# First layer of a two-layer decoder on one core: VectorE's second norm moved behind the next pair's masks, and ScalarE's first exponentials behind two copies

## The chip, the core and the metric

The kernel runs on one core of one Trainium2 chip. The metric is the device time of one execution in microseconds (us); the span of a profile runs from the first to the last recorded instruction. PE is TensorE (PEld its weight loads), DVE is VectorE, ACT is ScalarE, POOL is GpSimd, and SP is the engine whose queue issues most of the transfers.

## The reference, cut to what matters

Two decoder layers work on 32 sequences of 64 tokens with 256 channels. Only the first two blocks of the first layer matter here:

```
x = layernorm(x + L0_attn(x))        # local, causal: 16 heads; q and k centred and normed per head;
                                     # scores squared, masked, times v, divided by their sum
x = layernorm(x + L0_xattn(x, ctx))  # cross: q and k RMS-normed, softmax over each sequence's 64
                                     # context positions, times v, output projection with bias
x = layernorm(x + L0_ffn(x))         # 16 routed experts of which 4 are used, 2 shared ones
```

The second layer follows: grouped causal attention, a cross attention with 32 heads, and a mixture of 8 experts with 2 used.

## The kernel before, in words

Everything is f32. `layer0` works through 2048 tokens in 8 pairs of 128-token tiles, and in 10 rounds. Round i does three pairs at once: the local attention of pair i (`la(i)`), the cross attention of pair j = i - 1 (`xa(i)`), and the router's part of pair i - 2 (`router(i)`). All three exist in rounds 2 to 7. Round 1 has no router part, and rounds 8 and 9 have no local attention. A block barrier ends the layer; then the router decides and the expert stage begins.

The order of work on each engine is written out by hand, and the engines meet at semaphores only. Score tiles (for the local and for the cross attention) share four PSUM banks `SB`; two banks `OB` take the weighted sums; all projections and transposes go in turn through two banks `PJ` (class `Banks`), each of which has to be emptied by the engine named in `emptier` before it is filled again. `fill[i, s]` lists the projections that are done ahead for a later group of two pairs in round i at one of four places (`inputs(i, 0)` to `inputs(i, 3)`). The local queries `la_q` and keys `la_k` stand in rounds 0, 2 and 4, the local values `la_v` and the context's keys in rounds 1, 3 and 5, and `kv` tiles for the second layer in rounds 2, 4, 6 and 7. The "query rounds" of the change are those with `la_q` in `fill[i, 0]`; with cross attention there are two of them, rounds 2 and 4.

What one round does around the change, by engine:

- PE: the local scores of pair i into `SB` (line 166, `l_KL` and `l_QM`), `inputs(i, 0)`, a wait for the masks (`ls_used`), the cross scores of pair j (line 166, `l_QX` and `l_KX`), the transposes of the normed pair i - 2 for the router (`r_xtr`, line 834; they wait for `ln2_done` and for a `PJ` bank), the local weighted sums (line 879; they wait for the squared weights), `inputs(i, 1)`, the transposes of O, the router's logits, the local output projection (line 59, `l_wo`), `inputs(i, 2)` and the transposes of the cross weights (line 900; they wait for the exponentials), `inputs(i, 3)`, the cross weighted sums (line 925), the next queries, the cross output projection, the query sums (line 132), and then the local scores of the next round.
- DVE: the masks of pair i, four products of 128x512 (line 676, `l_W`), `inputs(i, 0)`, half of the cross softmax (lines 665 and 666), the outputs of the local attention, `inputs(i, 1)`, the other half, the router's logits, residual and moments, the first norm, the outputs of the cross attention, residual and moments, the query sums (lines 713 and 714), and last the second norm of pair j (`apply(j, 1, ...)`, line 657), which waits for POOL's root (`ln2_root`, line 398).
- ACT: squares of the masked scores (line 514), `inputs(i, 0)` (for `la_q` lines 471 and 473), the copy of `r_xtr` (line 495), the exponentials of the first two banks (`exps(j, (0, 1))`, line 505), `inputs(i, 1)` (for `la_k` lines 479 and 480), the copy of the turned O (line 524), `inputs(i, 2)`, and the other exponentials.
- POOL: at the end of the round the root for the query sums (line 439) and then the root of the second norm (lines 397 and 398).

Of the kernel before, what the change touches and what calls it, by code (L numbers as in the profile page):

```python
# [170 lines left out]
def layer0(nc, es, io, fx):  # L171
# [5 lines left out]
    def inputs_of(g):  # L177
        return {name: [(name, g, i) for i in range(n)] for name, n in
                (("la_q", 2), ("la_k", 2), ("la_var", 1), ("la_v", 2), ("xa_k", 2), ("xa_ks", 1), ("xa_kb", 1),
                 ("xa_v", 2))}  # L180

    fill = {(i, s): [] for i in range(-1, ROUNDS) for s in range(4)}
    for g in range(GROUPS):
        n, i = inputs_of(g), 2 * (g - 1)
# [38 lines left out]
    def la(i):  # L223
        return i < PAIRS

    def xa(i):
        return 0 <= i - 1 < PAIRS

    def router(i):
        return 0 <= i - 2 < PAIRS  # L230
# [21 lines left out]
    def count(name, per=1, step=1):  # L252
        return Count(es, nc, "l0_" + name, per, step)
# [10 lines left out]
    ln1_done, ln2_done = count("ln1_done", 2), count("ln2_done", 2)  # L264
    ln1_stats, ln2_stats, ln1_root, ln2_root = (count(n) for n in ("ln1_stats", "ln2_stats", "ln1_root", "ln2_root"))
# [3 lines left out]
    with ExitStack() as mem:  # L269
# [36 lines left out]
        with nc.Block() as block:  # L306
# [138 lines left out]
            def _(act):  # L445
# [47 lines left out]
                def turned_pair(use, dst):  # L493
                    pj.wait_full(act, use)
                    nc.scalar.activation(dst.rearrange("p m (t q) -> p t m q", t=2),
                                         pj.bank(use)[:].rearrange("p (t m q) -> p t m q", t=2, m=KC),
                                         ACT.Copy).then_inc(pj.emptied["A"], 1)

                def exps(j, which):
                    act.wait_ge(q_root.sem, q_root.at(j))  # L500
                    for r in which:
                        act.wait_ge(xs_used.sem, xs_used.at(j, r))
                        for t in range(2):
                            part = WX[:, r, t * PTOK:(t + 1) * PTOK]
                            last = nc.scalar.activation(part, part, ACT.Exp, scale=qs[:, j % 2, t:t + 1])
                        last.then_inc(xw_ready.sem, 1)

                inputs(-1, 0)
                for i in range(ROUNDS):
                    j = i - 1  # L510
                    if la(i):
                        for r in range(RG):
                            act.wait_ge(ls_used.sem, ls_used.at(i, r))
                            nc.scalar.activation(W[:, r], W[:, r], ACT.Square).then_inc(lw_ready.sem, 1)  # L514
                    inputs(i, 0)
                    if router(i):
                        turned_pair(("r_xtr", i - 2), XTA[:, :, (i - 2) * PTOK:(i - 1) * PTOK])
                    if xa(i):
                        exps(j, (0, 1))
                    inputs(i, 1)  # L520
                    if la(i):
                        use = ("la_otr", i)
                        pj.wait_full(act, use)
                        nc.scalar.activation(OT[:].rearrange("p a (c q) -> p c a q", c=2 * PER),
                                             pj.bank(use)[:].rearrange("p (c a q) -> p c a q", c=2 * PER, a=2),
                                             ACT.Copy).then_inc(pj.emptied["A"], 1)
                    inputs(i, 2)
                    if xa(i):
                        exps(j, (2, 3))
                        for r in range(RG):  # L530
                            act.wait_ge(pt_full.sem, pt_full.at(j, r))
                            nc.scalar.activation(WT[:, r].rearrange("p c q -> p (c q)"), SB[r][:],
                                                 ACT.Copy).then_inc(pt_used.sem, 1)
                    inputs(i, 2, True)
                    inputs(i, 3)
                    if la(i):
                        turned_pair(("xa_xtr", i), XT[:])
                    if xa(i):
                        turned_pair(("xa_otr", j), OT2[:])
                    if la(i):  # L540
                        use = ("xa_q", i)
                        pj.wait_full(act, use)
                        for m in range(KC):
                            got = pj.bank(use)[:, m * PTOK:(m + 1) * PTOK]
                            nc.scalar.activation(SQQ[:, m, :], got, ACT.Square, bias=cols[:, 0, m:m + 1])
                            last = nc.scalar.activation(QX[:, m, :], got, ACT.Identity, bias=cols[:, 0, m:m + 1])
                        last.then_inc(pj.emptied["A"], 1)

            @block.vector
            def _(dve):  # L550
# [102 lines left out]
                def apply(p, n, rooted, done):  # L653
                    dve.wait_ge(rooted.sem, rooted.at(p))
                    for t in range(2):
                        x = X[:, 2 * p + t, :]
                        nc.vector.tensor_scalar(x, x, mv[:, n, t, 0:1], rs[:, n, t:t + 1], ALU.subtract,
                                                ALU.mult).then_inc(done.sem, 1)
# [12 lines left out]
                for i in range(ROUNDS):  # L671
                    j = i - 1
                    if la(i):
                        dve.wait_ge(ls_full.sem, ls_full.at(i))
                        for r in range(RG):
                            nc.vector.tensor_tensor(W[:, r].rearrange("p (c q) -> p c q", q=SEQ),  # L676
                                                    SB[r][:].rearrange("p (c q) -> p c q", q=SEQ),
                                                    fx.cmask[:].unsqueeze(1).broadcast_to([P, 8, SEQ]),
                                                    ALU.mult).then_inc(ls_used.sem, 1)
                    inputs(i, 0)  # L680
                    if xa(i):
                        softmax(j, (0, 1))
                    if la(i):
                        g = i // 2
                        outputs(i, lo_full, lo_done, lambda t: O[:, t, :].rearrange("p (s j d) -> p j s d", s=2, d=16),
                                lambda t: dq[:, g % 2, 2 * (i % 2) + t].rearrange("p (j s) -> p j s", s=2))
                    inputs(i, 1)
                    if xa(i):
                        softmax(j, (2, 3))
                    if router(i):  # L690
                        use = ("r_logit", i - 2)
                        pj.wait_full(dve, use)
                        own(dve, nc.vector.transpose(sums[:, 0:2 * QUAD], pj.bank(use)[:, 0:2 * QUAD]))
                        nc.vector.tensor_copy(
                            fx.LG[:, pair_tiles(i - 2), :],
                            sums[:, 0:2 * QUAD].rearrange("p (t k) -> p t k", k=QUAD)[:, :, 0:E0]).then_inc(pj.emptied["D"], 1)
                    if la(i):
                        if i % 2 == 0:
                            dve.wait_ge(ld_x.sem, ld_x.at(i // 2))
                        moments(("la_out", i), i, 0, ln1_stats)  # L700
                    inputs(i, 2)
                    if la(i):
                        apply(i, 0, ln1_root, ln1_done)
                    inputs(i, 3)
                    if xa(i):
                        outputs(j, xo_full, xo_done, lambda t: O2[:, t, :].rearrange("p (j s d) -> p j s d", s=2, d=16),
                                None)
                        dve.wait_ge(biased.sem, biased.at(j))
                        moments(("xa_out", j), j, 1, ln2_stats)
                    if la(i):  # L710
                        use = ("xa_qs", i)
                        pj.wait_full(dve, use)
                        own(dve, nc.vector.transpose(sums[:, 0:2 * QUAD], pj.bank(use)[:, 0:2 * QUAD]))
                        nc.vector.tensor_scalar(qs[:, i % 2],
                                                sums[:, 0:2 * QUAD].rearrange("p (t k) -> p t k", k=QUAD)[:, :, 0],
                                                DIM * EPS_RMS, None, ALU.add).then_inc(pj.emptied["D"], 1)
                    if xa(i):
                        apply(j, 1, ln2_root, ln2_done)

            @block.tensor  # L720
            def _(pe):
# [2073 lines left out]
```

## Time and profile before

| | |
|---|---|
| runs of before, median (lowest to highest) | 1218.32 us (1214.48 to 1219.55) |
| profiled execution: its time, its span | 1217.71 us, 1215.5 us |
| mean granted TensorE clock | 0.967 of full speed |
| PE busy | 1084.9 us, 89% |
| PEld busy | 843.9 us, 69% |
| ACT, DVE, POOL busy | 501.1, 482.0, 442.9 us (41%, 40%, 36%) |
| rounds of the first layer | from about 44 us to 346 us of the span |

A busy share is an average over the whole span; the stage of the change is a quarter of it. A row of a timeline tells when a run of equal instructions started, how long it took, and in brackets how long its engine had been idle before it and what ended that. A granted clock of 1.00 is 2.4 GHz and one of 0.50 is 1.2 GHz.

### The profile page before, as it was taken

What the parts mean: (1) busy time and instruction counts of PE and PEld (TensorE: products, weight loads), DVE (VectorE), ACT (ScalarE), POOL (GpSimd) and SP (SyncE); (2) the same over time, 40 slices, a digit from 0 to 9 for tenths busy, and PEclk for the clock granted to TensorE, in tenths of its full rate; (3) what the DMA queues carried; (4) which work ended last, traced back from release to release, by engine and by line L of the source; (5) the groups of instructions that cost most, each with busy time, mean ns of one, the idle gap of its engine ahead of it and who ended that gap; (6) DMA issues with size and microseconds to landing.
All of it is one profiled execution on the core that took longest, in us unless ns stands there. A gap on an engine that the chain in (4) does not pass through costs nothing. (4 is left out here: it accounts for less than half of the span.)

```text
span 1215.5 us, 29092 instructions
## 1 busy us (share of the span) xinstructions
PE 1084.9 (89%) x10278; PEld 843.9 (69%) x10279; DVE 482.0 (40%) x1268; ACT 501.1 (41%) x1301; POOL 442.9 (36%) x565
## 2 busy tenths in 40 slices
PE   5887988888889899999987999988659999999997
PEld 2455665666545677777756787776538989999997
DVE  1355464655475133333335666663383000000422
ACT  1524445444534233333334666664304334333342
POOL 2023030031136886777736673333034200200433
PEclk9999899999999999999989999999769999999999
DMA  6069719021056455565472110000056755655672
GB/s 197 19 197 362 265 32 368 20 69 64 19 233 158 147 196 174 149 191 152 121 273 102 45 37 20 19 20 2 4 182 220 221 163 176 207 174 171 205 242 83
DMA packets 116521, 173.17 MB, mean 142 GB/s; under 512 B 17440, under 2 KB 94096, under 8 KB 114960
## 3 DMA queue, kind: packets, MB, share of 16 engines
q1 hardware_dynamic: 89936, 128.46, 32.9%
q0 software_dynamic: 9696, 26.75, 7.0%
q10 hardware_dynamic: 16784, 16.49, 4.1%
q8 instruction: 75, 1.23, 0.4%
q14 instruction: 30, 0.25, 0.1%
HBM read 105.07 MB, written 65.27 MB: 140 GB/s over the span
## 5 line engine op out<-in xcount | busy, mean ns | idle before, releaser
L2610 PE MATMUL bank<-m_XGT,m_w 128*128 128x128 f32 x1248 | 147.9, 277 | 0.0
L2610 PEld LDWEIGHTS bank<-m_XGT,m_w 128*128 128x128 f32 x1248 | 144.9, 194 | 1.2 <-issue 1.0
L2624 PE MATMUL bank<-w,m_HT 128*128 x624 | 141.0, 379 | 0.0
L2624 PEld LDWEIGHTS bank<-w,m_HT 128*128 128x128 f32 x624 | 115.7, 190 | 14.1
L2442 ACT ACTIVATE m_HT<-bank,m_b 128x128 f32<-128x128 f32 x312 | 89.0, 368 | 81.3 <-PE bank L2610 81.3
L1619 PE MATMUL bank<-m_W,m_XGT 128*128 x316 | 107.5, 463 | 0.0
L1476 ACT ACTIVATE m_XGT<-bank 128x256 f32<-128x256 f32 x79 | 30.3, 383 | 119.5 <-DVE m_US L1563 117.4
L2402 POOL DMA_INDIRECT m_GA<-ys,r_pos x32 | 31.8, 993 | 123.1 <-SPq L2357 114.1
L1233 POOL DMA_INDIRECT GA<-ys,r_pos x64 | 64.3, 1005 | 31.6 <-issue 17.7
L1555 DVE TENSOR_TENSOR m_H<-bank,m_SG 128x176 f32<-128x176 f32 x79 | 27.0, 341 | 118.8 <-ACT m_SG L1480 118.8
L1413 POOL DMA_INDIRECT xs<-X,r_pos x64 | 63.2, 988 | 25.8 <-issue 14.0
L397 POOL TENSOR_SCALAR l_rs<-l_mv 128x2 f32<-128x2 f32 x16 | 3.6, 225 | 189.3 <-DVE l_mv L650 189.1
L1619 PEld LDWEIGHTS bank<-m_W,m_XGT 128*128 128x128 f32 x316 | 54.0, 190 | 18.2 <-issue 0.9
L2388 POOL DMA_INDIRECT xs<-X,r_pos x32 | 31.8, 994 | 69.0 <-DMA xs<-X,r_pos 41.0
L2453 ACT ACTIVATE m_Y<-bank 128x256 f32<-128x256 f32 x39 | 15.0, 383 | 92.3 <-PE bank L2624 92.3
L1639 PE MATMUL bank<-m_W2A,inputs 128*128 x158 | 47.6, 383 | 1.7 <-ACT inputs L1485 0.8
L1852 ACT ACTIVATE l_WX<-bank 128x512 f32<-128x512 f32 x64 | 33.8, 604 | 35.1 <-PE bank L2107 35.1
L59 PE MATMUL bank<-XT,inputs 128*128 128x512 f32 x96 | 44.7, 613 | 2.7 <-ACT raw L467 1.3
L1641 PE MATMUL bank<-m_W2B,inputs 128*128 x158 | 47.0, 379 | 0.0
L1563 DVE COPY m_US<-bank 128x256 f32<-128x256 f32 x79 | 33.5, 425 | 33.5 <-PE bank L1641 31.1
L2526 DVE TENSOR_TENSOR X<-bank,X 128x512 f32<-128x512 f32 x8 | 5.5, 692 | 89.8 <-PE bank L2586 89.8
L514 ACT ACTIVATE l_W<-l_W 128x512 f32<-128x512 f32 x32 | 19.4, 630 | 45.8 <-DVE l_W L676 45.8
(379 smaller groups left out, 2265.0 us busy)
## 6 DMA issues: line engine op xcount, KB each, us to landing
m_w<-in_m_w SPq DMA_DIRECT2D x35, 1024.0 KB, 5.3
xs<-zeros SPq DMA_DIRECT2D x1, 10112.0 KB, 34.2
ys<-zeros SPq DMA_DIRECT2D x1, 10112.0 KB, 34.7
ys<-m_US ACTq DMA_DIRECT2D x79, 128.0 KB
m_GS<-xs SPq DMA_DIRECT2D x72, 128.0 KB, 2.2
w<-in_m_w SPq DMA_DIRECT2D x8, 1024.0 KB, 14.2
m_W<-in_w SPq DMA_DIRECT2D x2, 2816.0 KB, 13.0
xs<-zeros SPq DMA_DIRECT2D x1, 4992.0 KB, 19.8
```

What stands on the lines that cost most here:

```text
L59: last = nc.tensor.matmul(dst, stills[i], movings[i], start=i == 0, stop=i == n - 1)
L1233: pool.indirect_dma_start(out=fx.GA[:, t % 2 * (t < EARLY), k, :], out_offset=None, in_=fx.ys, in_offset=bass.IndirectOffsetOnAxis(ap=fx.p ...
L1413: pool.indirect_dma_start(out=fx.xs, out_offset=bass.IndirectOffsetOnAxis(ap=r.pos[:, t, k:k + 1], axis=0), in_=fx.X[:, t, :], in_offset=N ...
L1563: nc.vector.tensor_copy(Y[:, b % 2, :], BY[b % 2][:, 0:DIM]).then_inc(y_used, 1)
L1619: last = nc.tensor.matmul(BU[b % 2][:, 0:IW], XGT[:, b % 2, m * P:(m + 1) * P], W13[:, m, bass.ds(e, 1), :], start=m == 0, stop=m == KC - 1)
L1639: nc.tensor.matmul(BY[b % 2][:, 0:DIM], HT[:, b % 2, 0, :], W2A[:, bass.ds(e, 1), :], start=True, stop=False)
L1641: nc.tensor.matmul(BY[b % 2][:, 0:DIM], HT[:, b % 2, 1, :], W2B[:, bass.ds(e, 1), :], start=False, stop=True).then_inc(y_full, 1)
L1852: nc.scalar.activation(WX[:, t, r].rearrange("p m c q -> p (m c q)"), SB[r][:], ACT.Exp, scale=D32 ** -0.5).then_inc(x_used.sem, 1)
L2388: pool.indirect_dma_start(out=fx.xs1, out_offset=bass.IndirectOffsetOnAxis(ap=r.pos[:, t, k:k + 1], axis=0), in_=X[:, t, :], in_offset=Non ...
L2442: last = nc.scalar.activation(HT[:, b % 2, at, :], BU[i][:, c * P:(c + 1) * P], ACT.Gelu, bias=b1[:, b % WB, at:at + 1])
L2610: last = nc.tensor.matmul(BU[i][:, c * P:(c + 1) * P], w1[:, b, m, lo:lo + P], XGT[:, b % 2, m * P:(m + 1) * P], start=m == 0, stop=m == K ...
L2624: last = nc.tensor.matmul(BY[b % 2][:, 0:DIM], HT[:, b % 2, c, :], w2[:, bass.ds(e, 1), c, :], start=c == 0, stop=c == CH - 1)
```

## The change

On DVE the second norm of pair i - 2 leaves the end of round i - 1 and stands in round i behind the four masks. The order of all else is kept. In rounds 8 and 9, which have no masks, the order stays what it was. On ACT, in a round whose `fill[i, 0]` holds `la_q` (rounds 2 and 4), the first two banks' exponentials come after the copies of `la_k` and of the turned O instead of before them.

```diff
@@ ScalarE
                         turned_pair(("r_xtr", i - 2), XTA[:, :, (i - 2) * PTOK:(i - 1) * PTOK])
-                    if xa(i):
+                    queries_now = any(u[0] == "la_q" for u in fill[i, 0])
+                    if xa(i) and not queries_now:
                         exps(j, (0, 1))
                     inputs(i, 1)
                     if la(i):
...
                                              ACT.Copy).then_inc(pj.emptied["A"], 1)
+                    if xa(i) and queries_now:
+                        exps(j, (0, 1))
                     inputs(i, 2)
@@ VectorE
                                                     ALU.mult).then_inc(ls_used.sem, 1)
+                    if router(i):
+                        apply(i - 2, 1, ln2_root, ln2_done)
                     inputs(i, 0)
...
                                                 DIM * EPS_RMS, None, ALU.add).then_inc(pj.emptied["D"], 1)
-                    if xa(i):
-                        apply(j, 1, ln2_root, ln2_done)
```

## Rows read from the trace of the kernel before

**Rows 1.** Busy PE, PEld, DVE, ACT, POOL in the rounds; granted clock, DMA share, GB/s

```profile
44.00:346.00 302.00, 255.26 (x3352) 180.72 (x3350) 156.08 (x384) 136.74 (x264) 55.29 (x74) 0.97 0.42 142
```

**Rows 2.** Waits of PE from 112 to 300 us: sum, times, longest

```profile
PE bank L166 <- DVE l_W L676: 12.8, 6, 2.3
...
PE bank L834 <- ACT l_QM L473: 2.8, 2, 1.4
```

**Rows 3.** Timeline of PE, round 3: start, us, what, idle time before

```profile
149.75 1.21 PE L166 MATMUL bank<-l_QM,l_KL 32*64 32x128 f32 x64
150.89 3.72 PE L59 MATMUL bank<-l_wv,inputs 128*128 128x256 f32 x16
156.67 1.20 PE L166 MATMUL bank<-l_KX,l_QX 32*64 32x128 f32 x64 [2.06 <-DVE l_W L676]
158.26 0.90 PE L834 MATMUL bank<-ident,X 128*128 128x128 f32 x4 [0.40 <-DVE l_V L606]
159.09 3.43 PE L879 MATMUL bank<-l_V,l_W 128*64 128x68 f32 x64
```

**Rows 4.** Timeline of DVE, round 3

```profile
151.41 0.17 DVE L714 TENSOR_SCALAR l_qs<-l_sums 128x2 f32<-128x2 f32 x1
153.39 0.73 DVE L657 TENSOR_SCALAR X<-X,l_mv,l_rs 128x256 f32<-128x256 f32 x2 [1.82 <-POOL l_rs L398]
154.04 2.48 DVE L676 TENSOR_TENSOR l_W<-bank,cmask 128x512 f32<-128x512 f32 x4
...
159.98 0.69 DVE L665 TENSOR_REDUCE l_mx<-bank 128x8 f32<-128x512 f32 x1
```

**Rows 5.** Timeline of POOL, round 3

```profile
151.65 0.71 POOL L439 TENSOR_TENSOR l_qs<-l_qs,neghalf 128x2 f32<-128x2 f32 x1 [5.64 <-DVE l_qs L714]
...
152.65 0.71 POOL L398 TENSOR_TENSOR l_rs<-l_rs,neghalf 128x2 f32<-128x2 f32 x1
```

**Rows 6.** Timeline of DVE, the masks of round 1

```profile
81.47 2.48 DVE L676 TENSOR_TENSOR l_W<-bank,cmask 128x512 f32<-128x512 f32 x4 [0.66 <-PE bank L166]
```

**Rows 7.** Timeline of DVE, the second norm ahead of round 2

```profile
115.89 0.73 DVE L657 TENSOR_SCALAR X<-X,l_mv,l_rs 128x256 f32<-128x256 f32 x2 [1.94 <-POOL l_rs L398]
```

**Rows 8.** Timeline of PE, round 2

```profile
113.41 3.70 PE L59 MATMUL bank<-inputs,l_wqk 128*128 128x512 f32 x8
119.16 1.20 PE L166 MATMUL bank<-l_KX,l_QX 32*64 32x128 f32 x64 [2.05 <-DVE l_W L676]
121.74 1.08 PE L834 MATMUL bank<-ident,X 128*128 128x128 f32 x4 [1.38 <-ACT l_QM L473]
122.75 3.90 PE L879 MATMUL bank<-l_V,l_W 128*64 128x68 f32 x64
126.58 4.27 PE L59 MATMUL bank<-inputs,l_wqk 128*128 128x512 f32 x8
...
136.30 1.04 PE L900 MATMUL bank<-ident,l_WX 128*128 128x128 f32 x8
```

**Rows 9.** Timeline of PE: local weighted sums of rounds 4, 5 and 6

```profile
196.69 3.41 PE L879 MATMUL bank<-l_V,l_W 128*64 128x68 f32 x64
...
232.16 2.77 PE L879 MATMUL bank<-l_V,l_W 128*64 128x68 f32 x64
...
267.47 2.12 PE L879 MATMUL bank<-l_V,l_W 128*64 128x68 f32 x64
```

**Rows 10.** Busy time and granted clock behind round 2's stall (columns as in rows 1)

```profile
120.95:127.75 6.80, 6.01 (x70) 5.07 (x71) 3.96 (x11) 4.62 (x9) 0.00 (x0) 0.50 1.08 384
```

**Rows 11.** Timeline of ACT, round 2

```profile
123.85 1.73 ACT L505 ACTIVATE l_WX<-l_WX,l_qs 128x256 f32<-128x256 f32 x4
129.17 0.69 ACT L479 ACTIVATE raw<-bank,l_cbp 128x512 f32<-128x512 f32 x1 [3.59 <-PE bank L59]
...
132.04 0.60 ACT L524 ACTIVATE l_OT<-bank 128x512 f32<-128x512 f32 x1
```

**Rows 12.** Timeline of SP at the barrier behind the layer

```profile
346.58 0.81 SPq L1346 DMA_DIRECT2D m_W<-in_w  x2
```

## The prediction

> **What bounds the kernel now.** I read the busy time of the layer's rounds first, then who PE waited for, then the timelines of each engine round by round. PE is busy for 255.3 of the 302 us [rows 1], so about 47 us of the stage are PE idling; DVE, ACT and POOL are each idle for half of it or more. What is worth time here is therefore a wait of PE. The largest one is PE's wait ahead of the cross scores for DVE's masks: 12.8 us in six waits, one in each of rounds 2 to 7, 2.1 us on average and 2.3 at most [rows 2].
>
> Round 3 shows why. DVE has finished the query sums at 151.58. The local scores that it is to mask are there at 150.96 [rows 3]. But the second norm stands in front of the masks, and it waits 1.82 us for POOL's root, which ends at 153.36 [rows 4, 5]. The norm takes 0.73, and the masks go from 154.04 to 156.52. PE has run out of work at 154.61 and starts the cross scores at 156.67 [rows 3]. Round 1 has no second norm, and there the masks start as soon as the local scores are done [rows 6].
>
> **The change, VectorE.** No instruction is added or taken away. In each of the six rounds the masks lose what stands in front of them: 1.82 us of idle time and 0.73 of norm in round 3, 1.94 and 0.73 in round 2 [rows 4, 7]. The masks of round 3 would go from 151.6 to 154.1 and those of round 2 from 114.0 to 116.5, so about 2.5 us earlier. In both rounds that is before PE's own work ends, 154.61 [rows 3] and 117.11 [rows 8]: the stall goes wholly. The norm follows from 154.1 to 154.8. POOL's root is ready at 153.4, provided that it isn't slowed. What waits for the norm is `r_xtr` on PE, and behind it everything else of PE. PE gets there after the cross scores, at 155.9, a microsecond after the norm's end. So the moved norm costs nothing, and its cover is the 1.2 us of cross scores.
>
> What is late next differs by round, and I count each by it.
>
> Rounds 2 and 4: `r_xtr` waits for the bank of the first `la_q`, which ACT empties after its squares [rows 2, 8]. ACT's chain starts with the masks, so `r_xtr` moves by the masks' 2.5 us, and PE behind it too: 2 x 2.5 = 5.0.
>
> Rounds 3 and 5: `r_xtr` waits for DVE to empty a bank of `la_v` [rows 3]. DVE runs without a gap from the norm to the softmax at 159.98 [rows 4], and this run starts earlier only by the idle time that goes, 1.8 us; the norm's 0.73 is still in front of `la_v`. 2 x 1.8 = 3.6.
>
> Rounds 6 and 7 have only `kv` tiles there, so PE gains its stall: twice the average, 4.3.
>
> Sum: 12.9 us. This is the term without TensorE's clock.
>
> **The clock.** Behind the stall of round 2, PE was granted 1.2 GHz from 120.95 to 127.75 [rows 10]. It came after 2.05 us of idling, 1.2 of work and 1.38 of idling again [rows 8]. The local weighted sums took 3.90 us there, 3.43 in round 3, 3.41 in round 4, 2.77 in round 5, and 2.12 in round 6, where no fall came [rows 3, 8, 9]. PE is what the path follows here. In round 2 the sums would give back 1.8, `la_k` (4.27 against the 3.70 of the same eight matmuls of `la_q`) 0.6, and `r_xtr` (1.08 against some 0.66, as far as 0.90 in round 3 bounds it) 0.4, so 2.8. Round 3 would give 1.3, round 4 as much and 0.2 for `r_xtr`, so 1.5, and round 5 0.65. Together 6.3 us, if all four falls go. After the change the longest idle time left around the cross scores of rounds 2 to 5 is the wait for ACT in rounds 2 and 4, which shrinks to 0.9: the cross scores start 2.05 earlier and `r_xtr` 2.5. I take 5 of the 6.3, since where a fall comes isn't the same for every shift of the work, and one can turn up elsewhere.
>
> The Trainium skill (TensorE: Matmul & The Clock Gate, "Why this matters for your kernels") advises against idle gaps of over about 3 us between bursts. By that rule waits of 2 us cost no clock, and taking them away gives none back: the sum would be 12.9 us. The falls of rows 8 and 10 came behind shorter gaps than the rule names; the rule makes for the first rival below.
>
> **The change, ScalarE.** It touches rounds 2 and 4. In round 2 ACT does the four exponentials from 123.85 to 125.58, and then waits 3.59 us for PE's `la_k` [rows 11]. So they hold up nothing, and to move them gives nothing. After the change the exponentials could start in their old place 2.5 us earlier, at 121.3, and the first `la_k` comes at most 2.5 + 2.8 earlier, at 123.9. That leaves 2.6 us for 1.73 of exponentials. In their new place they start after the copy of O, at 132.6 in the times of before, and end at 134.4; PE transposes the first weights at 136.30 [rows 8, 11]. Cost nothing as well, covered by the output projection and a `kv` tile on PE. Without that cover it would be 1.73 twice, 3.5 us; without a gap for them in the old place, a gain of the same size. I take 0.
>
> **Sum.** 12.9 + 5 = 18 us off the profiled execution's 1217.7 (span 1215.5, 2.2 around it). The layer ends in a barrier at 346, behind which the experts' weights are first loaded [rows 12]; so what is won in the layer is kept whole, and what comes after is only shifted. The profiled time is 0.6 below the median of 1218.3, so I forecast 1218.3 - 18 = 1200.
>
> **Rivals.**
> - The clock gives nothing back: falls stay where they are, or others come in their place. 12.9 us, 1205. For it: 1.2 us of work stood between the two idle times ahead of round 2's fall, and what made the difference to rounds 6 and 7, which had the stall and no fall of the clock in their sums, the rows don't say [rows 9]. Against it: the falls of rounds 2 to 5 all lie right behind the stall that goes, and they are all that keeps the rounds' clock at 0.97 [rows 1].
> - Another wait takes over. DVE in rounds 3 and 5, or ACT in rounds 2 and 4, is now nearly full from the masks to the output projection; if half of each round's gain is lost there, 6 to 8 us stay: 1211. Against it: in round 3 DVE's chain is already counted at its smaller 1.8, and round 1 shows such a round with no stall.
> - No change. The stall on PE is hidden by a later wait for something that doesn't move. It would need such a wait in every round, and the barrier row leaves only DVE, ACT or a transfer. Transfers are triggered by the same rounds and shift with them. 1218.
> - The other side: the second norm becomes late. Its end decides `r_xtr`, and the weighted sums, the projections and all of PE queue behind that. It has 1.0 us of slack against the cross scores' end; from there on each us counts in six rounds. It would first have to eat the 2.1 us won, and 1 us more in each round gives 1224. That takes a norm 4 us later than reckoned, by POOL's root slowed beside the masks. Round 3's two roots took 0.71 us each beside an idle DVE, and all of POOL's work from the query sums to the second norm 1.7 us [rows 4, 5]; the masks beside it would have to stretch that to over 5 us. The Trainium skill (GPSIMD Engine Reference, "Key points") says that GpSimd shares its SBUF interfaces with VectorE and contends with DVE instructions that have two SBUF inputs or run in a 2-port mode. A mask has one PSUM and one SBUF input, so by that sentence it would not; no row here has the root of the norm beside the masks.
>
> **How the numbers follow.** Main case (stall and most of the clock) 0.62; clock gives nothing 0.25; another wait 0.07; no change 0.04; slower 0.02. The range for 8 in 10: upward to the clock rival's 1205, and 4 us for two or three clock falls elsewhere (one cost 0.65 to 2.8 in the sums above), 1209; downward all 6.3 of the clock, 1199, and the 4 us by which runs of the same kernel lie below their median, 1195. About 0.5% of the time, 6.1 us, is what a measurement can tell from no change. Faster by over 0.5% (below 1212.2): the first two cases and most of the third, 0.93; within 0.5% 0.05; slower by over 0.5% 0.02.
>
> **What the profile after would show.** Right: PE's wait for the masks is gone in rounds 2 to 7 or is a few tenths. The masks start at once behind the query sums, the second norm behind them with no wait for POOL. `r_xtr` waits for ACT or for DVE's `la_v`, not for the norm. The exponentials of rounds 2 and 4 stand behind the copy of O and no transpose waits for them. The barrier comes at about 328 instead of 346, with the clock of the layer near 1.00. Clock rival: the barrier at 333, with weighted sums of over 3 us still there. Wrong: a wait of PE for the norm (line 657's successor) of over 1 us in each round, or waits for the exponentials ahead of the transposes; or a barrier that moves as forecast and a time that doesn't, by more clock falls in the expert stages.

## The result and the profile after

| | before | after |
|---|---|---|
| median of six runs (lowest to highest) | 1218.09 us (1214.48 to 1219.55) | 1198.91 us (1196.98 to 1202.31) |
| profiled execution: time, span | 1217.71, 1215.5 us | 1198.34, 1196.5 us |
| clock of the whole run | 0.967 | 0.972 |

The ratio is 0.9853, with a 95% interval of 0.983 to 0.9876. The forecast was 1200 us, in a range of 1195 to 1209.

PE's waits in the kernel after from 112 to 282 us, which is rounds 2 to 6 and the cross scores of round 7 (sum in us, times, longest), the view of rows 2:

```profile
PE bank L820 <- POOL l_ks L429: 3.1, 2, 1.6
PE bank L837 <- DVE l_O L639: 2.2, 5, 0.6
PE bank L132 <- ACT l_KL L480: 1.8, 2, 0.9
PE bank L837 <- ACT l_QM L473: 1.6, 2, 1.0
PE bank L132 <- ACT l_SQK L461: 1.2, 1, 1.2
PE bank L837 <- DVE l_V L609: 1.0, 2, 0.6
```

The wait for the masks, 12.8 us and first in [rows 2], isn't there any more. Of what stands in the list only the fifth row is new; the wait for DVE's values (the sixth) has grown, in round 3 from 0.40 us [rows 3] to 0.59. The timeline of DVE in round 3, against [rows 4]:

```profile
147.47 0.17 DVE L719 TENSOR_SCALAR l_qs<-l_sums 128x2 f32<-128x2 f32 x1
147.55 2.48 DVE L679 TENSOR_TENSOR l_W<-bank,cmask 128x512 f32<-128x512 f32 x4
149.94 0.73 DVE L660 TENSOR_SCALAR X<-X,l_mv,l_rs 128x256 f32<-128x256 f32 x2
150.58 0.18 DVE L608 COPY l_V<-l_rk 64x32 f32<-64x32 f32 x1
```

That of PE, against [rows 3]:

```profile
145.82 1.21 PE L166 MATMUL bank<-l_QM,l_KL 32*64 32x128 f32 x64
146.96 3.72 PE L59 MATMUL bank<-l_wv,inputs 128*128 128x256 f32 x16
150.61 1.21 PE L166 MATMUL bank<-l_KX,l_QX 32*64 32x128 f32 x64
152.41 0.63 PE L837 MATMUL bank<-ident,X 128*128 128x128 f32 x4 [0.59 <-DVE l_V L609]
152.96 2.12 PE L882 MATMUL bank<-l_V,l_W 128*64 128x68 f32 x64
```

And that of POOL, against [rows 5]:

```profile
148.71 0.72 POOL L398 TENSOR_TENSOR l_rs<-l_rs,neghalf 128x2 f32<-128x2 f32 x1
```

The masks start behind the query sums, the norm behind them with no idle time, and the cross scores follow PE's values at once. POOL's root takes 0.72 beside the masks; it was 0.71 beside an idle DVE. PE turns the normed pair (line 837) when DVE has emptied a bank of values, 1.7 us after the norm's end. The weighted sums (line 882) take 2.12 us instead of 3.43.

The rounds of the layer by busy time and granted clock, against [rows 1]:

```profile
core 0: us, PE busy (x) PEld busy (x) DVE busy (x) ACT busy (x) POOL busy (x), PEclk, DMA share, GB/s
44.00:328.00 284.00, 249.68 (x3416) 175.44 (x3400) 156.48 (x387) 136.26 (x264) 55.39 (x74) 1.00 0.45 151
```

PE's clock is 1.00 throughout these rounds. The barrier lies at 328.5, where it was at 346.6:

```profile
328.54 0.81 SPq L1349 DMA_DIRECT2D m_W<-in_w  x2
```

From the start of round 2's local scores to PE's first matmul behind the barrier, 234.33 us became 214.73 (112.27 to 346.60 before, 113.83 to 328.56 after): 19.6 us less. The part in front was 1.56 us longer in this execution and the part behind about 0.95 shorter, neither by the change; 19.60 - 1.56 + 0.95 is the 19.0 us between the spans.

### The profile page after: what moved, and what is told of

Read it like the earlier page. It is cut to its first block and busy times, and to the rows that moved or that the text cites. A ratio compares the mean times of both kernels' runs of the same rounds, so it can differ in the third digit from the quotient of the medians.

```text
span 1196.5 us, 29092 instructions
## 1 busy us (share of the span) xinstructions
PE 1079.2 (90%) x10278; PEld 838.5 (70%) x10279; DVE 481.5 (40%) x1268; ACT 501.3 (42%) x1301; POOL 443.1 (37%) x565
## 5 line engine op out<-in xcount | busy, mean ns | idle before, releaser
L59 PE MATMUL bank<-inputs,l_wqk 128*128 128x512 f32 x64 | 31.6, 638 | 3.0 <-ACT l_QM L473 1.6
```

The source lines that it names most:

```text
L59: last = nc.tensor.matmul(dst, stills[i], movings[i], start=i == 0, stop=i == n - 1)
```

## The experiments

Every ratio is against runs of the kernel before taken beside the experiment. Those beside experiments 1, 2, 3 and 5 had a median of 1220.90 us, those beside 4, 6, 7 and 8 one of 1215.66, so across these two groups only ratios and lengths of rounds are compared. Where rounds are compared, they run from the start of one round's local scores on PE (line 166, `l_QM`) to the next.

**1. VectorE's part alone.** The change without the ScalarE edit:

```diff
+                    if router(i):
+                        apply(i - 2, 1, ln2_root, ln2_done)
...
-                    if xa(i):
-                        apply(j, 1, ln2_root, ln2_done)
```

> Only VectorE's part of the change; ScalarE's exponentials stay in front of the key copies in rounds 2 and 4. Theory (all of the gain is the masks' advance, the exponentials stand in an idle gap of ScalarE in either place): the same time as the whole change, 1198.9 us within a few us, ratio to before 0.985, and the gap of ScalarE ahead of the first key copy of round 2 is about 0.6 us where it was 2.36 with the whole change. Rival (with the masks earlier, the exponentials in their old place hold up the key copies): 1.7 us or less lost in each of two rounds, so up to 3.5 us, 1202.

1200.86 us, ratio 0.9855 (0.9822 to 0.9889): the same as the whole change. ScalarE in round 2 of this run:

```profile
121.84 1.73 ACT L505 ACTIVATE l_WX<-l_WX,l_qs 128x256 f32<-128x256 f32 x4
124.35 0.69 ACT L479 ACTIVATE raw<-bank,l_cbp 128x512 f32<-128x512 f32 x1 [0.78 <-PE bank L59]
```

and in the kernel after:

```profile
125.23 0.69 ACT L479 ACTIVATE raw<-bank,l_cbp 128x512 f32<-128x512 f32 x1 [2.36 <-PE bank L59]
...
128.58 1.70 ACT L505 ACTIVATE l_WX<-l_WX,l_qs 128x256 f32<-128x256 f32 x4
132.56 0.60 ACT L461 ACTIVATE XT<-bank 128x512 f32<-128x512 f32 x1 [2.28 <-PE bank L59]
```

In their old place the exponentials end 0.78 us before the first key copy can start, so they hold up nothing; in the new place they end 2.28 before ScalarE's next work. Round 2 is 32.13 us long here (112.80 to 144.93) and 31.99 with both parts; round 4, the other one that the edit touches, 32.31 and 32.30.

**2. ScalarE's part alone.** The other half of the change, with the second norm in its old place:

```diff
-                    if xa(i):
+                    queries_now = any(u[0] == "la_q" for u in fill[i, 0])
+                    if xa(i) and not queries_now:
                         exps(j, (0, 1))
...
+                    if xa(i) and queries_now:
+                        exps(j, (0, 1))
```

> Only ScalarE's part of the change. Theory: no effect, 1218 us, ratio 1.000 within 0.3%; PE still waits 2.1 us for the masks in each of rounds 2 to 7. Rival 1 (the exponentials held up work before): up to 3.5 us less, 1214.5. Rival 2 (moved behind the output copy they come too late for the transposes of the weights): a wait of PE for them in rounds 2 and 4 and up to 3.5 us more.

1220.74 us, ratio 1.0007 (0.9986 to 1.0027). PE's wait for the masks is 12.7 us in six, as before. The edit does nothing for the time that can be told from the noise, with the VectorE edit or without.

**3. Four extra matmuls in the stall.** The order of before, with PE at work instead of idle ahead of the cross scores of rounds 2 to 7. The extra results go into a bank that is written anew before it is read.

```diff
                         if la(i):
+                            if router(i):
+                                pe.wait_ge(xo_done.sem, xo_done.at(i - 2, 1))
+                                busy(nc, OB[0], fx.ident[:], 4)
                             pe.wait_ge(ls_used.sem, ls_used.at(i, RG - 1))
```

> The order of before, but PE does four extra matmuls of 128x512 into a free bank (their result is overwritten) where it would wait for the masks in rounds 2 to 7: some 1.85 us of work in stalls of 2.05 to 2.3. The masks come no earlier. Theory of the clock (idle time at the stall is what makes TensorE fall to 1.2 GHz in rounds 2 to 5): the falls are gone, the local weighted sums take 2.1 us in each of those rounds, and up to 6.3 us are won with the stall still counted, 1212. Rival (the falls have another cause, or come in another place of the rounds): weighted sums of 3.4 to 3.9 us remain and the time is 1218. If the filler overruns the stall it costs up to 0.5 us a round.

1216.39 us, ratio 0.9976 (0.9956 to 0.9996). Round 2 of this run:

```profile
118.18 3.60 PE L145 MATMUL bank<-ident 128*128 128x512 f32 x8
121.70 1.21 PE L166 MATMUL bank<-l_KX,l_QX 32*64 32x128 f32 x64
...
123.67 2.11 PE L882 MATMUL bank<-l_V,l_W 128*64 128x68 f32 x64
```

The expectation had the clock right and the filler wrong. All six weighted sums take 2.1 us and no fall is left in the rounds. But one f32 matmul of 128x512 stands as two records in the trace and took 0.90 us; I had read the eight records of `la_q` in 3.70 us as eight matmuls. So the four overran the stall: the cross scores of round 2 start 1.3 us later after its local scores than before. By the lengths of the rounds that cost 4.2 us against experiment 4, most of it in rounds 3 and 5 to 7, and ate more than half of the gain.

**4. Two extra matmuls.** The same edit with 2 in place of 4.

> As the filler run, with two extra matmuls instead of four: the four took 3.60 us by that run's trace, 0.90 each, and so overran the stall of 2.05 us by 1.3 in each round; two take 1.8 and fit. The stall stays as long as it was, only busy. Theory of the clock: no fall of the clock in rounds 2 to 7, weighted sums of 2.1 us, the rounds as before but for these, so 5 to 6.3 us less than before, ratio 0.995, and the rest of the way to the whole change, 13 us, is the masks' advance. Rival (it took more filling than that, or the gain of the four came from something else than the clock): falls in some rounds and under 2 us won.

1210.6 us, ratio 0.9959 (0.9944 to 0.9975). PE in round 2, 3 and 5:

```profile
117.38 1.88 PE L145 MATMUL bank<-ident 128*128 128x512 f32 x4
119.45 1.21 PE L166 MATMUL bank<-l_KX,l_QX 32*64 32x128 f32 x64 [0.20 <-DVE l_W L676]
122.12 0.63 PE L834 MATMUL bank<-ident,X 128*128 128x128 f32 x4 [1.46 <-ACT l_QM L473]
122.68 2.12 PE L882 MATMUL bank<-l_V,l_W 128*64 128x68 f32 x64
...
156.41 2.11 PE L882 MATMUL bank<-l_V,l_W 128*64 128x68 f32 x64
...
226.23 2.11 PE L882 MATMUL bank<-l_V,l_W 128*64 128x68 f32 x64
```

The masks come as late as before, and PE still waits 0.20 us for them behind the filler. From round 2 to the barrier it is 227.29 us, 7.0 less than before: this is the clock alone. The second gap, the 1.46 us wait for ScalarE in round 2, did not have to be filled for it. From here to the kernel after it is 12.6 more: this is the masks' advance with the clock already up.

**5. The norm further back.** The whole change, with the second norm behind the first half of the softmax instead of in front of it:

```diff
-                    if router(i):
-                        apply(i - 2, 1, ln2_root, ln2_done)
                     inputs(i, 0)
                     if xa(i):
                         softmax(j, (0, 1))
+                    if router(i):
+                        apply(i - 2, 1, ln2_root, ln2_done)
```

> The whole change, but the second norm goes further back, behind the first two banks' softmax instead of in front of it. It tests the slack of the norm, 1 us by the rows. Theory (its end decides when PE turns the normed pair, and the weighted sums and all of PE queue behind that): by the rows of the profile after, the turn starts 3 us later in rounds 2 and 4, 5 in rounds 3 and 5 and 3.5 in rounds 6 and 7, 23 us in all, with the clock falling again behind these waits: 1220 to 1228, as slow as before or slower. Rival (PE's order behind it has slack of its own, and the delay is absorbed further on): 1199 to 1205.

1231.17 us, ratio 1.0107 (1.0062 to 1.0152), slower than either kernel. PE in round 3, and its wait in round 4:

```profile
153.53 1.21 PE L166 MATMUL bank<-l_KX,l_QX 32*64 32x128 f32 x64
159.84 1.12 PE L837 MATMUL bank<-ident,X 128*128 128x128 f32 x4 [5.11 <-DVE X L660]
160.89 3.90 PE L882 MATMUL bank<-l_V,l_W 128*64 128x68 f32 x64
...
198.57 0.66 PE L837 MATMUL bank<-ident,X 128*128 128x128 f32 x4 [3.47 <-DVE X L660]
```

The six waits for the norm are 3.49, 5.11, 3.47, 4.94, 3.47 and 3.48 us, 24.0 in all where 23 were reckoned, and round 8 has a seventh of 3.47 that I had left out. The clock falls again behind some of them, as the 3.90 shows, and not behind others: in round 4 the transposes behind the wait took 0.66 us and the weighted sums 2.11. From round 2 to the barrier it is 30.8 us more than after. So the rival of the late norm names a real mechanism; the change as made stays 1 us on the safe side of it.

**6. The whole change again**, unaltered, beside the runs with two extra matmuls and with the early memsets.

> The whole change, unaltered, beside the others on the same chip. Ratio to before 0.985; its difference to the run with two extra matmuls is the worth of the masks' advance without the clock, 12.9 us by the prediction's sum.

1200.7 us, ratio 0.9871 (0.9855 to 0.9886). It is 9.9 us below the run with two extra matmuls by the medians, where the rounds alone say 12.2 (227.29 against 215.11). The part behind the barrier differs between executions by more than these 2.3 us: from PE's first matmul there to the end it took 866.7 us in the one profile and 870.5 in the other. The lengths of the rounds are the sharper measure here: rounds 2 to 5 of this profile and of the first one of the whole change agree within 0.02 us each. By the times this repeat is 15.0 us below the kernel before, where the first comparison gave 19.2; the two ratios' intervals overlap.

**7. POOL's memsets earlier.** The kernel after has one long wait that before had not. ScalarE in its round 6:

```profile
255.73 0.60 ACT L461 ACTIVATE l_SQK<-bank 128x512 f32<-128x512 f32 x1 [1.95 <-DMA kv<-l_SQK]
```

SP's queue ahead of that, and below it the same issues in the kernel before:

```profile
248.31 1.93 SPq L345 DMA_DIRECT2D inputs<-in_w  x4
250.28 2.66 SPq L349 DMA_DIRECT2D S<-in_w  x4
252.99 0.90 SPq L360 DMA_DIRECT2D kv<-l_SQK  x2
```

```profile
262.85 1.92 SPq L345 DMA_DIRECT2D inputs<-in_w  x4
264.81 1.87 SPq L349 DMA_DIRECT2D S<-in_w  x4
266.79 0.83 SPq L360 DMA_DIRECT2D kv<-l_SQK  x2
```

ScalarE can't reuse a staging buffer before its `kv` tile is stored. The store stands in SP's queue behind eight loads of shared weights, which wait for two memsets of POOL, and these stand at the start of POOL's round 6, behind the root of the second norm. So the loads start 4.2 us after the round's local scores in both kernels (258.62 before, 244.09 after), and they and the two stores behind them are issued 9.0 us after these before and 9.8 after. What moved is ScalarE: it would be free for this copy 9.7 us after the local scores instead of 12.1.

```diff
-                    if i == PAIRS - 2:
-                        pj.wait_full(pool, ("xa_v", GROUPS - 1, 1))
-                        nc.gpsimd.memset(fx.S13[:, :, :, HS:], 0.0)
-                        nc.gpsimd.memset(fx.S2[:, SC - 1, :], 0.0).then_inc(fx.padded, 1)
...
                                                 ALU.add).then_inc(biased.sem, 1)
+                        if i == PAIRS - 3:
+                            pj.wait_full(pool, ("xa_v", GROUPS - 1, 1))
+                            nc.gpsimd.memset(fx.S13[:, :, :, HS:], 0.0)
+                            nc.gpsimd.memset(fx.S2[:, SC - 1, :], 0.0).then_inc(fx.padded, 1)
```

> The whole change, and POOL's two small memsets for the padding of the shared weights come at the end of round 5 instead of the start of round 6. In the profile after, ScalarE waits 1.95 us in round 6 for the store of a kv tile, which sits in SP's queue behind eight loads of shared weights, and these wait for the memsets; PE loses 1.2 us there. Theory: the loads go out some 7 us earlier, ScalarE's wait for the store and PE's for ScalarE are gone, and 0.9 us are won, too little for the timed ratio but plain in the length of round 6: 27.8 us from local scores to local scores instead of 28.7. Rival (the store is late for another reason): the wait stays.

1197.51 us, ratio 0.9843 (0.9828 to 0.9859). The same copy of ScalarE now waits for PE only:

```profile
255.74 0.60 ACT L461 ACTIVATE l_SQK<-bank 128x512 f32<-128x512 f32 x1 [0.86 <-PE bank L59]
```

Round 6 takes 27.74 us (245.18 to 272.92), against 28.71 in the first profile of the whole change and 29.07 in the second. The mechanism is shown. How much of the time it is worth is not settled: the medians of runs taken together are 3.2 us apart and all five runs lie below all four of the whole change, but the rounds show only 1.3 of it, and the intervals of the ratios overlap.

**8. And the key sums' root first.** With the memsets early, POOL takes the root of the key sums ahead of the first norm's root in the four rounds that have one:

```diff
-                    if la(i):
+                    keyed = any(u[0] == "xa_ks" for s in range(4) for u in fill[i, s])
+                    if la(i) and not keyed:
                         norm_root(i, 0, ln1_stats, ln1_root)
...
                                                         ALU.pow).then_inc(k_root.sem, 1)
+                                norm_root(i, 0, ln1_stats, ln1_root)
```

> The whole change, the early memsets, and in rounds 0, 1, 3 and 5 POOL takes the root of the key sums before the root of the first norm. There PE waits 1.56 us for the key sums' root, which stands behind 0.95 us of the norm's root. Theory: PE's wait falls to about 1.0 us, 0.6 won in each of rounds 1, 3 and 5, the first norm comes 1.3 us later and is covered by VectorE's 3.4 us of waiting for the context's values; with the memsets some 2.5 to 3 us below the whole change, 1196. Rival (the first norm, now late, holds up VectorE or the transposes that need it): no faster than the whole change or slower, with a wait of PE for the first norm in those rounds.

1197.55 us, ratio 0.9843 (0.9828 to 0.9857). PE's wait falls from 1.56 to 0.96 us, and round 3 is 32.46 us long (146.60 to 179.06) instead of 33.06:

```profile
166.93 1.13 PE L822 MATMUL bank<-ident,l_ks 128*128 128x128 f32 x8 [0.96 <-POOL l_ks L426]
```

From round 2 to the barrier it is 212.56 us, the shortest of all and 1.2 less than with the memsets alone: 0.6 in each of rounds 3 and 5. In the time, 1197.55 us against 1197.51, it isn't seen. The part behind the barrier was 4.5 us longer in its profiled execution than in the other's (871.0 against 866.5), and a difference like that can hide a gain of this size.

## Why the prediction was right, step by step

Gains in us from round 2 on, by the lengths of the rounds. The clock's column is before against two extra matmuls, the masks' column these against after:

| round | masks' advance, forecast | measured | clock, forecast | measured |
|---|---|---|---|---|
| 2 | 2.5 | 2.65 | 2.8 | 2.84 |
| 3 | 1.8 | 1.93 | 1.3 | 1.48 |
| 4 | 2.5 | 2.53 | 1.5 | 1.58 |
| 5 | 1.8 | 2.08 | 0.65 | 1.00 |
| 6 | 2.15 | 1.31 | 0 | 0.07 |
| 7 to the barrier | 2.15 | 2.06 | 0 | 0.07 |
| sum | 12.9 | 12.6 | 6.3, taken as 5 | 7.0 |

**The masks' advance** is right in place and size, and so is what comes next: ScalarE's chain in rounds 2 and 4, DVE's values in rounds 3 and 5. The rule for rounds 3 and 5, that only the idle time counts and not the norm, held: against experiment 4, and counted from the local scores, the masks start 2.6 us earlier in round 3, DVE's values 1.9, and the round gained 1.93. Round 6 is the one miss. I had counted PE's stall as its gain, and with it reckoned that "transfers are triggered by the same rounds and shift with them". The loads of round 6 did shift with the round, and so stayed at the same place in it, while ScalarE reached the copy behind them 2.4 us sooner in the round. Experiment 7 took the wait away and gave back 1.0 to 1.3 us.

**The clock** gave more than I took. The four falls of before went, none came in another place of the rounds, and in round 5 the slower cross scores (1.64 against 1.2 us) had been left out of the term:

```profile
229.55 1.64 PE L166 MATMUL bank<-l_KX,l_QX 32*64 32x128 f32 x64 [2.06 <-DVE l_W L676]
```

Experiment 4 shows the cause: PE's idling at the stall, and not the lateness of the masks. The rival in which the clock gives nothing back is refuted. The size is that of one execution: against the profile of experiment 2, which has the same stalls, the rounds of experiment 4 are 8.4 us shorter and not 7.0.

**The Trainium skill's rule** on gaps of over about 3 us (TensorE: Matmul & The Clock Gate, "Why this matters for your kernels") would have left the sum at 12.9 us and the time at 1205. The measurement decides against it here: waits of 2.1 to 2.3 us, with a second one of 1.38 behind them in rounds 2 and 4 only, cost 7 us of clock in the execution profiled, and filling the first with 1.88 us of work took all of it away. Nor did waits longer than the rule's 3 us always bring a fall: that of 3.47 in round 4 of experiment 5 brought none.

**ScalarE's edit** costs and gives nothing, as forecast (experiments 1 and 2). In their old place the exponentials were reckoned to have 2.6 us for their 1.73, so 0.9 to spare; experiment 1 shows 0.78.

**The moved norm** is never what PE waits for directly, and its root isn't slowed beside the masks (0.72 us). Against the cross scores it has the slack of 1 us that the forecast gave it: it ended at 150.67 and they at 151.82. In rounds 3 and 5 that slack is not the whole account, though. PE waits there for DVE's values (0.59 us in round 3), and these stand behind the norm, so a norm that had to wait for its root would have delayed PE at once. The forecast has the norm's 0.73 us in that chain, but not in its rival of the late norm. No run delayed the norm in this place. Experiment 5 shows what a norm too far back costs.

**1200 forecast, 1198.9 measured.** In the rounds, clock and masks together gave 0.4 us more than 12.9 + 6.3, and 1.6 more than the 18 that I took. The median of before was 0.4 us above the time profiled and that of after 0.6 above its own, so the two profiles are typical of their runs. That the forecast time was met within 1.1 us is in part luck: the parts of the run outside these rounds differ by some us between executions, and the repeat of experiment 6 gained 15.0 us. The forecasts for each round are the firmer test.

## What to carry to other kernels

Ask of each wait in an engine's written order what stands behind it, and whether its data has long been there. A short operation that waits for a slow helper does no harm where it is, but everything behind it does; put the work that another engine needs first, and move the waiting operation no further back than its own reader allows: here 1 us of slack was enough, and with the norm further back, waits of 3.5 to 5 us cost 31 in all, the clock included. When one engine comes earlier in its round, look for a queue whose issues stay where they were: it becomes the next wait. And a stall on TensorE may cost half as much again as its length (here 12.8 us of stalls and 7.0 of clock), since it can take the clock down with it; filling the stall with throwaway work separates the two.

## What the runs showed of the hardware

The clock fell to 1.2 GHz right behind single idle gaps of 2.1 us, and the same gap did not always bring a fall. In the profile of before rounds 2 to 5 had a fall and rounds 6 and 7 none; in that of experiment 2, with the same stalls, round 7 had one as well. PE had been busy there from 289.5 to 294.4, idle for 2.08 us, and was granted 0.50 of its clock from 298.4 to 299.5:

```profile
296.46 1.96 PE L166 MATMUL bank<-l_KX,l_QX 32*64 32x128 f32 x64 [2.08 <-DVE l_W L679]
298.36 1.11 PE L837 MATMUL bank<-ident,X 128*128 128x128 f32 x4
299.40 2.39 PE L882 MATMUL bank<-l_V,l_W 128*64 128x68 f32 x64
```

The cross scores took 1.96 us there instead of 1.20, the transposes 1.11 instead of 0.64. Longer gaps didn't always bring one either: behind 3.47 us in round 4 of experiment 5 all was at full speed. What made the difference no run here shows. So a profile of one execution shows what a fall costs there, and a few us of the clock's term are the luck of the execution.
